# Sparse attention block with expert mixing: the order of the query tiles in the second pass, 4, 7, 5, 6 in place of 7, 4, 6, 5

## The chip, the cores and the metric

The kernel runs on one core of a Trainium2 chip. The metric is the device time of one execution in microseconds (us), the median of several runs. Before the change it is 866.75 us (three runs, 865.97 to 867.92). The engines that matter here are TensorE (PE: matmuls and transposes; its weight loads are the rows PEld), VectorE (DVE), ScalarE (ACT), GpSimd (POOL) and SyncE (SP), whose queue issues the transfers.

## The reference

One block over 1024 tokens of width 512: a layer norm, then the sum of the input, a latent attention with 32 heads and a low-rank expert mix. The attention keeps for each query only the 128 keys that an indexer with 16 heads scores highest.

```python
xn = layernorm(x)                                       # 1024 x 512
q_lat = rmsnorm(xn @ q_a_w) ; q = q_lat @ q_b_w         # 32 heads, 128 plain + 64 rotated
ckv = xn @ kv_a_w ; k_nope, v = rmsnorm(ckv[:, :64]) @ kv_b_w
idx_scores = sum_n iw[n] * relu(iq[n] @ ik.T)           # causal
mask = top_k(idx_scores, 128) & causal                  # one mask for all heads
scores = (q_nope @ k_nope.T + q_pe @ k_pe.T) * 192**-0.5
attn = softmax(where(mask, scores, -inf))
out = x + (attn @ v) @ o_w + sum_e gate[e] * (xn @ A[e].T) @ Bm[e].T * 0.5
```

## The kernel before

The 1024 queries are eight tiles of 128 rows. Causality makes query tile t meet t + 1 blocks of 128 keys, so tile 4 has rows of 640 keys, tile 5 of 768, tile 6 of 896 and tile 7 of 1024. The attention works in latent space: of each head it keeps a 128-wide query (64 latent, 64 rotated) in two float16 parts, high and low, and three products of parts give float32 quality.

The heads go in pairs, 16 pairs. There are two passes over the pairs: the first (half 0, units 0 to 15, steps 0 to 127) does query tiles 0 to 3, the second (half 1, units 16 to 31, steps 128 to 255) tiles 4 to 7. A unit is one pair in one pass and has eight steps: step s of a unit (s = 0 to 7) is head s % 2 of the tile that `ORDERS[half][s // 2]` names. So the list has one entry for two steps, and `tile_of(g)` (L266) is the only way in which it sets widths, and `op` and the index in `out_T` (L767) follow it.

The order of the work is written out by hand, one program for each engine, with semaphores between them. In the second pass, for step g, with the names that the document uses from here on:

- TensorE (loop at L777): S(g+3), the scores of three steps ahead, six matmuls at L731 in one of two score banks; then for an even step T(g), the transposes of its probabilities (L788, one a key block, in two chunks: four blocks, then the rest); then at s = 1 the job R (L647 to L651, five matmuls, the rotated query part of unit u+2), at s = 5 the job L (the same lines, the latent part), at s = 7 the job O (L767, four transposes of the last unit's output); then V, the products with the values (L758, three a key block), of step g-2 for an even step and of step g-4 for an odd one.
- VectorE (loop at L1367): M(g+3), the masked scores with their row minimum of the negated values (L1297, followed by L1302 on odd steps); then P(g), the low parts of T(g)'s chunks (L1075); then R's or L's or O's second reading (L1342, L1075). At s = 4 the last unit's output is scaled (L1313, L1320, L1325).
- ScalarE: the high parts of T(g) (L835), then the exponential of step g+2 (L1024).
- GpSimd: for the odd steps, whose probabilities are transposed by DMA, the split in two parts (L1567, L1569), and the rotation of the queries (L1535, L1540, L1542, L1547), for which SyncE swaps rows by DMA (L425, L426). SyncE issues the DMA transposes (L478) and places the queries (L435).

Three rules tie the engines. S(g) waits until M(g-2) has read the bank (L724). M(g) waits until the probabilities of step g-4 are out of its buffer: for an even step their transposes, for an odd step the low part from GpSimd (L1289 to L1294). And all T chunks, R, L and O go in turn through two banks, psT[0] and psT[1] (`RING`, L327 to L345): each waits until the use before it in its bank has been read (`wait_freed`, L695). A unit has eleven uses: T0a, T0b, R, T2a, T2b, T4a, T4b, L, T6a, T6b, O. So R waits for P of T0a, L for P of T4a, T6b for the reading of L, O for P of T6a, and T0b of the next unit for the reading of O. These numbers after S, M, T, V and P are the step in its unit, and a dash (S0', S3') means the next unit.

Of the kernel before, what the change touches and what calls it, by code (L numbers as in the profile page):

```python
# [47 lines left out]
OUT_S = O_S * WVO_S  # L48
assert HW_S * B_S == OUT_S

ORDERS = ([3, 0, 2, 1], [7, 4, 6, 5])
GROUPS = [[3, 2, 1], [5, 4], [7, 6]]
CH = 512
ARENA = 17024
# [7 lines left out]
def block_kernel(nc, x, wcat, wik, wiq, qbT, wkT, wvT, qpe, ow, bm, qnorm, kvnorm, rbias,  # L62
                 cosq, sinq, cosk, sink, ident_d, causal_d, out):
    with ExitStack() as ctx:
# [192 lines left out]
        def half_of(g):  # L257
            return g // (8 * NP)
# [7 lines left out]
        def tile_of(g):  # L266
            return ORDERS[half_of(g)][g % 8 // 2]

# [268 lines left out]
        def _(pe):  # L537
# [224 lines left out]
            def out_T(bank, u):  # L762
# [3 lines left out]
                for j in range(4):  # L766
                    last = nc.tensor.transpose(bank[:, j * P:(j + 1) * P], op[:, ORDERS[c].index(4 * c + j), :], ident[:])  # L767
                last.then_inc(ot_mm, 1)
# [888 lines left out]
```

## Time and profile before

| | |
|---|---|
| median of three runs | 866.75 us |
| the profiled execution, its own time | 866.68 us |
| its span in the profile | 864.9 us, so 1.8 us lie around it |
| TensorE busy, share of the span | 790.0 us, 91% |
| VectorE busy | 658.2 us, 76% |
| ScalarE busy | 586.3 us, 68% |
| GpSimd busy | 559.8 us, 65% |
| TensorE clock granted | 0.99 of full, mean |

The span is a chain of stages: projections and indexer up to about 285 us, the first pass to about 467 us, the second pass to about 769 us, then the output products. Busy shares are means over all of them. In the timeline a TensorE row "x6" is six matmuls in a row, and its end is modelled: the time that a group takes from its neighbours is the distance from its start to the start of the group behind it. A bracket at the end of a row gives the idle time of the engine ahead of it and what ended it.

### The profile page before, as it was taken

To read this page: it belongs to the slowest core of one execution; us is meant where nothing else is said; L and a number is where in the kernel's file an instruction comes from. 1 tells how busy PE (TensorE), PEld (TensorE's weight loads), DVE (VectorE), ACT (ScalarE), POOL (GpSimd) and SP (SyncE) were. 2 spreads that over 40 slices of the span, in tenths; PEclk is the share of its full clock that TensorE was granted. 3 is DMA by queue.
4 is the path that set the end of the run, shared out by engine and by line. 5 is a ranking of instruction groups with operands and counts; after the bars stand their busy time and mean duration, and the time that the engine had idled before them with its cause. 6 is when DMAs were issued, how large, how long until landed. Compare 5 with 4: busy or idle time off the path is not lost.

```text
span 864.9 us, 20146 instructions
## 1 busy us (share of the span) xinstructions
PE 790.0 (91%) x7432; PEld 489.1 (57%) x7432; DVE 658.2 (76%) x1558; ACT 586.3 (68%) x1325; POOL 559.8 (65%) x478
## 2 busy tenths in 40 slices
PE   4999999978767989898987999999999999999998
PEld 2556545434434555555554677767767767764443
DVE  6367688899998999999998888888887888841000
ACT  3687799979886878888886767666776666740000
POOL 3177398968885676676676788878788888640000
PEclk9999999989999999999999999999999999999999
DMA  8022211213433655655654577777688888861110
GB/s 263 26 74 74 62 55 57 67 25 96 139 109 97 161 136 148 165 135 153 158 147 116 108 152 147 152 152 140 132 147 151 144 154 145 178 129 49 49 49 24
DMA packets 185697, 100.85 MB, mean 117 GB/s; under 512 B 133632, under 2 KB 159616, under 8 KB 185600
## 3 DMA queue, kind: packets, MB, share of 16 engines
q1 hardware_dynamic: 185600, 99.57, 49.9%
q8 instruction: 59, 0.97, 0.5%
q14 instruction: 38, 0.31, 0.1%
HBM read 36.62 MB, written 6.29 MB: 50 GB/s over the span
## 4 chain that ended last, share of the span: by engine, by line
POOL 32%; PE 24%; issue 13%; DVE 12%; DMA 8%; SPq 8%; ACT 3%; POOLq 0%; DVEq 0%; ACTq 0%
PE psS L804 10%; DMA arena<-arena 7%; SPq L478 5%; POOL bias L1516 5%; POOL arena L1542 4%; POOL arena L1540 4%; PE psT L602 4%; POOL arena L1547 3%; PE psS L615 3%; DVE m L1232 3%; POOL ikT L1569 3%; POOL arena L1569 3%; DVE bias L1239 2%; POOL bias L1569 2%; SPq L425 2%
## 5 line engine op out<-in xcount | busy, mean ns | idle before, releaser
L731 PE MATMUL psS<-keyT,arena 128*128 128x512 f16 (+3 forms) x1152 | 230.1, 328 | 7.4 <-DVE small L1297 4.0
L835 ACT ACTIVATE arena<-psT 128x512 f16<-128x512 f32 (+3 forms) x344 | 162.0, 502 | 102.2 <-PE psT L788 64.2
L1297 DVE CUSTOM_DVE_ANT_0 arena<-psS,bias 128x512 f32<-128x512 f32 (+7 forms) x256 | 191.4, 751 | 36.0 <-PE psS L731 16.1
L1024 ACT ACTIVATE arena<-arena,small 128x512 f32<-128x512 f32 (+7 forms) x256 | 197.5, 774 | 29.6 <-DVE small L1297 24.0
L1075 DVE SCALAR_TENSOR_TENSOR arena<-psT,arena 128x512 f16<-128x512 f32 (+3 forms) x262 | 135.2, 536 | 24.4 <-ACT arena L835 23.9
L731 PEld LDWEIGHTS psS<-keyT,arena 128*128 128x128 f16 x1152 | 91.8, 98 | 71.8 <-issue 13.3
L615 PE MATMUL psS<-ikT,big 128*128 128x512 f16 (+3 forms) x528 | 103.8, 341 | 23.0 <-DVE bias L1165 20.9
L788 PE MATMUL psT<-ident,arena 128*128 128x128 f32 x672 | 105.2, 277 | 17.0 <-DVE arena L1075 9.5
L1516 POOL TENSOR_TENSOR bias<-arena,bias 128x768 f32<-128x768 f32 (+2 forms) x48 | 91.4, 1909 | 25.4 <-ACT arena L905 14.7
L788 PEld LDWEIGHTS psT<-ident,arena 128*128 128x128 f32 x672 | 77.3, 141 | 45.0 <-ACT arena L1024 29.1
L615 PEld LDWEIGHTS psS<-ikT,big 128*128 128x128 f16 x528 | 49.3, 100 | 72.3 <-DVE bias L1165 28.4
L1239 DVE MATCH_REPLACE8 bias<-m,bias 128x768 f32<-128x768 f32 (+4 forms) x112 | 89.9, 809 | 0.0
L1232 DVE MAX8 m<-bias 128x8 f32<-128x768 f32 (+4 forms) x112 | 87.5, 816 | 0.5
L1540 POOL TENSOR_TENSOR arena<-arena,sq 128x512 f32<-128x512 f32 x32 | 40.8, 1276 | 65.5 <-DMA arena<-arena 65.5
L758 PEld LDWEIGHTS psO<-val,arena 128*128 128x128 f16 x1728 | 66.1, 98 | 10.7 <-DVE arena L1075 1.6
L758 PE MATMUL psO<-val,arena 128*128 128x64 f16 x1728 | 69.5, 193 | 0.8 <-DVE arena L1075 0.8
L835 ACT ACTIVATE big<-psT 128x512 f16<-128x512 f32 (+1 forms) x64 | 36.2, 566 | 45.4 <-PE psT L767 32.0
L835 ACT ACTIVATE arena<-arena 128x512 f16<-128x512 f32 (+1 forms) x112 | 62.7, 591 | 0.2 <-DMA arena<-in_wiq 0.2
L1422 POOL TENSOR_TENSOR arena<-arena 128x512 f16<-128x512 f32 x32 | 37.5, 1174 | 38.4 <-ACT arena L835 38.4
L1075 DVE SCALAR_TENSOR_TENSOR big<-psT,big 128x512 f16<-128x512 f32 (+1 forms) x64 | 41.8, 653 | 26.8 <-ACT big L835 26.8
L1547 POOL TENSOR_TENSOR arena<-arena 128x512 f16<-128x512 f32 x32 | 37.1, 1160 | 37.4 <-ACT arena L835 37.2
L1165 DVE SCALAR_TENSOR_TENSOR bias<-psS,arena,bias 128x512 f32<-128x512 f32 (+3 forms) x64 | 45.1, 746 | 14.1 <-ACT psS L928 13.6
(165 smaller groups left out, 1404.1 us busy)
## 6 DMA issues: line engine op xcount, KB each, us to landing
arena<-arena SPq DMA_DIRECT2D x192, 128.0 KB, 2.4
arena<-in_wiq SPq DMA_DIRECT2D x32, 256.0 KB, 2.8
arena<-in_ow SPq DMA_DIRECT2D x16, 512.0 KB, 3.8
arena<-in_qbT SPq DMA_DIRECT2D x16, 256.0 KB, 2.5
wvo_parts<-arena SPq DMA_DIRECT2D x16, 256.0 KB, 2.2
arena<-in_qpe SPq DMA_DIRECT2D x16, 128.0 KB, 3.0
arena<-in_x SPq DMA_DIRECT2D x8, 256.0 KB, 2.9
out<-arena SPq DMA_DIRECT2D x8, 256.0 KB, 2.0
```

What stands on the lines that cost most here:

```text
L615: last = mm(bank[:, c:c + w], iq[:, a, n, t * P:(t + 1) * P], ikT[:, b, c:c + w], start=(a, b) == (0, 0), stop=(a, b) == (1, 0))
L731: last = mm(bank[:, k:k + w], Q[:, u % 2, h, a, q:q + P], keyT[:, b, h, k:k + w], start=(a, b) == (0, 0), stop=(a, b) == (1, 0))
L758: last = mm(dst, src[:, a, j * P:(j + 1) * P], val[:, b, j, :], start=j == 0 and n == 0, stop=j == nb - 1 and n == 2)
L788: last = nc.tensor.transpose(bank[:, (j % 4) * P:(j % 4 + 1) * P], pr_of(g)[:, j * P:(j + 1) * P], ident[:])
L804: mm(psS[u][:, 0:CH], big[:, a, n, ds(t * P, P)], wvo[n][:, b, :], start=n == 0 and (a, b) == (0, 0), stop=False)
L835: return nc.scalar.activation(dst, src, ACT.Copy, scale=scale)
L1024: nc.scalar.activation(pr_of(g)[:, 0:kw], pr_of(g)[:, 0:kw], ACT.Exp, bias=shift[:, g % 8:g % 8 + 1], scale=-1.0, accum_out=rsum[:, unit_o ...
L1075: return v.scalar_tensor_tensor(out=dst, in0=src, scalar=scale, in1=hi, op0=ALU.mult, op1=ALU.subtract)
L1232: v.max(m8[:, slot], bias[:, TOFF[t]:TOFF[t + 1]]).then_inc(tk_max, 1)
L1239: v.match_replace(out=row, in_to_replace=m8[:, slot], in_values=row, imm_value=TAKEN).then_inc(tk_rep, 1)
L1297: v.tensor_tensor_reduce(out=pr_of(g)[:, 0:kw], in0=bank[:, 0:kw], in1=bias[:, TOFF[t]:TOFF[t + 1]], scale=-c_s, scalar=3e38, op0=ALU.add, ...
L1516: g.tensor_tensor(row, src[:, 0:P * (t + 1)], row, ALU.add).then_inc(sum_done, 1)
```

## The change

One list changes; every other line is the same.

```diff
-ORDERS = ([3, 0, 2, 1], [7, 4, 6, 5])
+ORDERS = ([3, 0, 2, 1], [4, 7, 5, 6])
```

In the second pass steps 0 and 1 of a unit now have tile 4 (5 key blocks) in place of 7 (8 blocks), steps 2 and 3 tile 7, steps 4 and 5 tile 5, steps 6 and 7 tile 6. The jobs R, L and O keep their steps. Each engine issues the same instructions in all.

On TensorE, ahead of the job O. First before: S1' (tile 7), T6, V4, S2' (tile 4), then O at L767.

```order
L731 MATMUL psS<-keyT,arena 128x512 x6
L788 MATMUL psT<-ident,arena 128x128 x6
L758 MATMUL psT<-val,arena 128x64 x21
L731 MATMUL psS<-keyT,arena 128x512
L731 MATMUL psS<-keyT,arena 128x128
L731 MATMUL psS<-keyT,arena 128x512
L731 MATMUL psS<-keyT,arena 128x128
L731 MATMUL psS<-keyT,arena 128x512
L731 MATMUL psS<-keyT,arena 128x128
L767 MATMUL psT<-ident,arena 128x128 x4
```

The same place of the changed kernel: S1' (tile 4), T6, V4, S2' (tile 7), then O.

```order
L731 MATMUL psS<-keyT,arena 128x512
L731 MATMUL psS<-keyT,arena 128x128
L731 MATMUL psS<-keyT,arena 128x512
L731 MATMUL psS<-keyT,arena 128x128
L731 MATMUL psS<-keyT,arena 128x512
L731 MATMUL psS<-keyT,arena 128x128
L788 MATMUL psT<-ident,arena 128x128 x7
L758 MATMUL psT<-val,arena 128x64 x18
L731 MATMUL psS<-keyT,arena 128x512 x6
L767 MATMUL psT<-ident,arena 128x128 x4
```

The wide scores stood ahead of T6 and now stand behind it, directly ahead of O; the transposes are seven in place of six and the value products 18 in place of 21.

On TensorE, ahead of the job R, before: the last matmul of S3 (tile 4), T0, V6 of the unit before, S4 (tile 6), R's first matmul.

```order
L731 MATMUL psS<-keyT,arena 128x128
L788 MATMUL psT<-ident,arena 128x128 x8
L758 MATMUL psT<-val,arena 128x64 x18
L731 MATMUL psS<-keyT,arena 128x512
L731 MATMUL psS<-keyT,arena 128x384
L731 MATMUL psS<-keyT,arena 128x512
L731 MATMUL psS<-keyT,arena 128x384
L731 MATMUL psS<-keyT,arena 128x512
L731 MATMUL psS<-keyT,arena 128x384
L647 MATMUL psT<-qlT,w1hi 128x512
```

The same place of the changed kernel: S3 (tile 7), T0, V6, S4 (tile 5), R's first matmul.

```order
L731 MATMUL psS<-keyT,arena 128x512 x6
L788 MATMUL psT<-ident,arena 128x128 x5
L758 MATMUL psT<-val,arena 128x64 x21
L731 MATMUL psS<-keyT,arena 128x512
L731 MATMUL psS<-keyT,arena 128x256
L731 MATMUL psS<-keyT,arena 128x512
L731 MATMUL psS<-keyT,arena 128x256
L731 MATMUL psS<-keyT,arena 128x512
L731 MATMUL psS<-keyT,arena 128x256
L647 MATMUL psT<-qlT,w1hi 128x512
```

Between S3 and R the transposes are now five in place of eight and S4 is one key block narrower.

On VectorE, at the turn of a unit, before: M1', P(T6) in two chunks, M2', the reading of O, M3', P(T0).

```order
L1297 ISA arena,small<-psS,bias 128x1024
L1297 ISA small 128x1
L1302 TENSOR_SCALAR small<-small 128x1
L1075 SCALAR_TENSOR_TENSOR arena<-psT,arena 128x512
L1075 SCALAR_TENSOR_TENSOR arena<-psT,arena 128x256
L1297 ISA arena,small<-psS,bias 128x640
L1297 ISA small 128x1
L1075 SCALAR_TENSOR_TENSOR big<-psT,big 128x512
L1297 ISA arena,small<-psS,bias 128x640
L1297 ISA small 128x1
L1302 TENSOR_SCALAR small<-small 128x1
L1075 SCALAR_TENSOR_TENSOR arena<-psT,arena 128x512 x2
```

The same place of the changed kernel.

```order
L1297 ISA arena,small<-psS,bias 128x640
L1297 ISA small 128x1
L1302 TENSOR_SCALAR small<-small 128x1
L1075 SCALAR_TENSOR_TENSOR arena<-psT,arena 128x512
L1075 SCALAR_TENSOR_TENSOR arena<-psT,arena 128x384
L1297 ISA arena,small<-psS,bias 128x1024
L1297 ISA small 128x1
L1075 SCALAR_TENSOR_TENSOR big<-psT,big 128x512
L1297 ISA arena,small<-psS,bias 128x1024
L1297 ISA small 128x1
L1302 TENSOR_SCALAR small<-small 128x1
L1075 SCALAR_TENSOR_TENSOR arena<-psT,arena 128x512
```

The 1024-wide minimum stood ahead of P(T6) and now stands ahead of P(T0).

## Rows read from the trace of the kernel before

**Rows 1.** Windows: busy us and count of each engine, granted clock, DMA share, GB/s
```profile
515.00:735.00 220.00, 218.47 (x2848) 155.19 (x2847) 181.72 (x398) 151.64 (x315) 181.53 (x143) 1.00 0.78 146
```
**Rows 2.** Timeline, VectorE, output scaling of two units: start us, us, instruction
```profile
599.88 0.19 DVE L1313 RECIPROCAL small<-small 128x8 f32<-128x8 f32 x1
600.36 0.69 DVE L1325 TENSOR_TENSOR arena<-psO,small 128x512 f32<-128x512 f32 x1
600.97 1.22 DVE L1297 CUSTOM_DVE_ANT_0 arena<-psS,bias 128x1024 f32<-128x1024 f32 x1
...
619.15 0.69 DVE L1325 TENSOR_TENSOR arena<-psT,small 128x512 f32<-128x512 f32 x1
```
**Rows 3.** Timeline, TensorE, the turn of a unit, from S1' to R
```profile
601.71 1.46 PE L731 MATMUL psS<-keyT,arena 128*128 128x512 f16 x6
603.00 0.82 PE L788 MATMUL psT<-ident,arena 128*128 128x128 f32 x6
603.66 0.78 PE L758 MATMUL psT<-val,arena 128*128 128x64 f16 x21
604.27 0.98 PE L731 MATMUL psS<-keyT,arena 128*128 128x512 f16 x6
605.39 0.66 PE L767 MATMUL psT<-ident,arena 128*128 128x128 f32 x4
...
606.32 0.98 PE L731 MATMUL psS<-keyT,arena 128*128 128x512 f16 x6
607.13 1.04 PE L788 MATMUL psT<-ident,arena 128*128 128x128 f32 x8
...
608.54 1.30 PE L731 MATMUL psS<-keyT,arena 128*128 128x512 f16 x6
609.67 0.38 PE L647 MATMUL psT<-qlT,w1hi 128*128 128x512 f16 x1
```
**Rows 4.** Timeline, VectorE, M ahead of P, tile 7 and tile 6
```profile
603.31 1.23 DVE L1297 CUSTOM_DVE_ANT_0 arena<-psS,bias 128x1024 f32<-128x1024 f32 x1 [0.52 <-PE psS L731]
604.65 1.01 DVE L1075 SCALAR_TENSOR_TENSOR arena<-psT,arena 128x512 f16<-128x512 f32 x2
...
612.81 1.09 DVE L1297 CUSTOM_DVE_ANT_0 arena<-psS,bias 128x896 f32<-128x896 f32 x1 [1.07 <-POOL arena L1569]
...
614.01 0.88 DVE L1075 SCALAR_TENSOR_TENSOR arena<-psT,arena 128x512 f16<-128x512 f32 x2
```
**Rows 5.** Timeline, first pass, a job R that waited for VectorE
```profile
357.72 0.10 PEld L647 LDWEIGHTS psT<-qlT,w1hi 128*128 128x128 f16 x1 [0.62 <-DVE arena L1075]
357.72 0.39 PE L647 MATMUL psT<-qlT,w1hi 128*128 128x512 f16 x1 [0.24 <-DVE arena L1075]
...
357.95 0.38 PE L648 MATMUL psT<-qlT,w1hi 128*128 128x512 f16 x1
```
**Rows 6.** Timeline, where the passes meet: M(128), S(130), O's reading, R
```profile
472.46 1.23 DVE L1297 CUSTOM_DVE_ANT_0 arena<-psS,bias 128x1024 f32<-128x1024 f32 x1
...
473.75 0.99 PE L731 MATMUL psS<-keyT,arena 128*128 128x512 f16 x6 [1.62 <-DVE small L1297]
...
476.07 0.69 DVE L1075 SCALAR_TENSOR_TENSOR big<-psT,big 128x512 f16<-128x512 f32 x1 [0.23 <-ACT big L835]
...
479.12 0.38 PE L647 MATMUL psT<-qlT,w1hi 128*128 128x512 f16 x1
```
**Rows 7.** Timeline, TensorE, the last two jobs O of the second pass's loop
```profile
752.43 0.98 PE L731 MATMUL psS<-keyT,arena 128*128 128x512 f16 x6
753.75 0.66 PE L767 MATMUL psT<-ident,arena 128*128 128x128 f32 x4 [0.34 <-DVE arena L1075]
...
768.21 0.66 PE L767 MATMUL psT<-ident,arena 128*128 128x128 f32 x4 [0.64 <-DVE arena L1075]
```
**Rows 8.** Timeline, GpSimd, the rotation behind its swap, the next split
```profile
601.95 1.27 POOL L1540 TENSOR_TENSOR arena<-arena,sq 128x512 f32<-128x512 f32 x1 [1.75 <-DMA arena<-arena]
...
605.55 1.65 POOL L1569 TENSOR_TENSOR bias<-arena,bias 128x768 f16<-128x768 f32 x1
```

## The prediction

> **What bounds the kernel now.** I read the busy shares of the page first: TensorE leads with 91% over the whole span. Since the list rules the second pass alone, I then read a window inside it: of 220 us TensorE is busy 218.47, at the full granted clock, 1.00, which is the 2.4 GHz level; VectorE is busy 181.72 and GpSimd 181.53 [rows 1]. So TensorE bounds this stage, and the other two have 17% to spare: whether they make it wait depends on where their work stands, not on how much there is. The timeline of VectorE gives the length of a unit: output scaling at 600.36 and at 619.15, 18.79 us apart [rows 2], and all units from 16 to 29 repeat it.
>
> Then I read the timeline of TensorE through the turn of a unit and took each group's cost from its start to the next start. Scores of tile 7 cost 1.29, of tile 4 0.81, of tile 6 1.13, so 0.16 a key block and 0.97 for tile 5; six transposes cost 0.66, so 0.11 a block; 21 value products 0.61, so 0.029 each [rows 3]. The only group that costs more than this is S2' ahead of O: tile 4, but 605.39 - 604.27 = 1.12, so TensorE stands 0.31 us in each unit [rows 3]. What it waits for: O's bank is free when P has read the first chunk of T6, and P stands behind M1' on VectorE. From the end of S1' at 603.00, M1' starts 0.31 later, P 1.34 after that at 604.65; its first chunk of 512 takes 0.69 (the length of such a reading in rows 6), to 605.34; O starts 0.05 later [rows 3, 4]. This chain is 2.39 us long, and TensorE has only 0.66 + 0.61 + 0.81 = 2.08 of work beside it. The difference is the stall.
>
> **The change, part by part.** It issues nothing new: matmuls, readings, exponentials, splits and transfers are as many and as wide. So at best it gives back stalls, and there is 0.31 in a unit. What is to be worked out is each such race in the new order. A chain is 0.31 + M and its turn + 0.69 + 0.05.
>
> O. Ahead of it M1' is now of tile 4. A block costs M 1.23 - 1.09 = 0.14 [rows 4], so three fewer save 0.42 and the chain is 1.97. TensorE has T6 of 7 blocks 0.77, V4 of 18 0.53 and S2' of tile 7 1.29, together 2.59. No stall: the 0.31 goes.
>
> R. It waits for P of T0a, which stands behind M3, now of tile 7: the chain is 2.39. TensorE has T0 of 5 blocks 0.55, V6 of 21 0.61 and S4 of tile 5 0.97: 2.13. It had 0.88 + 0.53 + 1.13 = 2.54, and was not late. So a new stall of 0.26.
>
> L. It waits for P of T4a behind M7, now of tile 6. M to P takes 614.01 - 612.81 = 1.20 [rows 4], the chain 2.25; TensorE has 0.66 + 0.70 + 0.81 = 2.17 (T4 of 6, V2 of 24, S0' of tile 4). A new stall of 0.08.
>
> T6b. It waits for VectorE's reading of L, which now comes late: behind S7 the chain is 0.31 + 1.20, P(T4) 0.93 or less, the output scaling 600.97 - 599.88 = 1.09 [rows 2], M0' of tile 4 0.74, the reading 0.69 and 0.05, together 5.01. TensorE needs 2.17 + 0.08 + 1.08 + 0.44 + 0.81 + 0.44 = 5.02. That is a dead heat; I take 0.02 for it and keep 0 and 0.1 as its ends.
>
> A stalled start. Does TensorE lose more than the wait when it restarts? In the first pass one R waited for VectorE: weight load and matmul both start at 357.72, and the next matmul 0.23 later, where 0.22 is usual [rows 5]. I take 0.01 at most, inside the rounding above. The Trainium skill, "TensorE: Matmul & The Clock Gate", section "Architectural detail: the array is 16× 32×32, not 1× 128×128", says that the queue pulls weight loads ahead of running matmuls, but also that a matmul can begin before its weight load is complete. By the first half alone each new stall would pay one more load, the 0.10 of rows 5, and the sum would be some 2.7 us higher; the row is with the second half.
>
> Waits that go but give nothing: VectorE idles 1.07 ahead of M5 for GpSimd's split of step 1 [rows 4]. With tile 4 in place of 7 there the split is done before its scores are; TensorE did not wait for this M, since S7 comes later. The next things late are R and L, as above.
>
> Per unit: 0.26 + 0.08 + 0.02 = 0.36 in place of 0.31. Over the pass: before, 14 stalls of 0.31 (units 16 to 29) and one of 753.75 - 752.43 - 0.81 = 0.51 in unit 30 [rows 7], together 4.85. After, R in units 17 to 29, 13 x 0.26 = 3.4, and L with T6b in units 16 to 29, 14 x 0.10 = 1.4; unit 30 has neither R nor L, and its O isn't late. Together 4.8: a gain of 0.05, nothing.
>
> Where the passes meet. S(128) starts as before but is 0.48 shorter, which brings the first pass's last readings, the masks and M(128) forward, and M(128) is 0.42 shorter: S(130), at 473.75 before [rows 6], starts at 472.85. Then S(130) and S(131) are of tile 7. Step 127 belongs to the first pass, where the readings come ahead of the next M, so M(130) stands behind the reading of O. O ends at 472.85 + 1.29 + 0.22 + 0.44 = 474.80; ScalarE and the reading add some 0.8 and 0.6, to 476.2 (476.07 + 0.6 before [rows 6]); M(130) takes 1.14 and M(131) with its turn 1.34, to 478.7; P(T0a) 0.69 and 0.05: R starts at 479.4, a full 1.0 us after TensorE is ready, where before it started at 479.12 [rows 6]. Up to R the new order has done less: 2 x 0.81 + 2 x 1.29 + 0.97 + 0.55 = 5.72 against 2 x 1.29 + 2 x 0.81 + 1.13 + 0.88 = 6.21. So it is 0.3 + 0.49 = 0.8 us behind. I take 0.8, with 0 and 1.4 as ends (a reading more or less in the way).
>
> The end. The last O waited 0.64 for VectorE behind two exponentials [rows 7], of tile 5; they are of tile 6 now, a block wider each, and one evacuation is a block narrower: 0.1 to 0.3, I take 0.2. The four value products of late steps are as long in all, and what comes behind them is untouched.
>
> **The sum**, against the profiled execution's own 866.68 us (span 864.9 and 1.8 around it, 0.07 under the median, so no correction): 866.68 - 0.05 + 0.8 + 0.2 = 867.6 us.
>
> **The rivals.**
> *A, the stall is simply gone.* If R and L hide after all, the pass gives back 4.85: 866.68 - 4.85 + 1.0 = 862.8 us. For it: VectorE and GpSimd idle, and O's is the only stall of a steady unit. Against it: the chain into R is the very chain of rows 3 and 4, and the work beside it is 0.26 too short, whatever the load.
>
> *B, slower by GpSimd's loop.* The rotation waits for its swap by DMA, which stands behind the transposes of step 3 on SyncE's queue, now of tile 7 in place of 4. It started at 601.95, 4.37 ahead of S3' at 606.32; the split of step 7 ended at 607.20 [rows 8], and M3' was due at 606.32 + 0.81 + 0.31 = 607.44: 0.24 to spare. The split is a block wider now, about 0.4, and M3' due 0.48 later, so 0.3 to spare. It decides from the point where the rotation starts less than 4.1 us ahead of S3'; from there M3' and so R are late by each further tenth, in 13 units. For it: the transposes are 8 blocks in place of 5 just ahead of the swap. Against it: those of step 1 are 5 in place of 8, also ahead of the swap, so its queue holds the same in all. At 0.25 a unit: 867.6 + 3.3 = 870.9 us.
>
> *C, the races are lost by more.* Each new stall costs 0.1 more (a restart, or T6b late): 27 x 0.1 = 2.7, 870.3 us. Rows 5 speak against it, the dead heat at T6b for it.
>
> *D, nothing moves:* the place where the passes meet costs nothing, 866.8 us. It lies in the forecast's own range.
>
> **How the numbers follow.** The bound from which this kernel can be told from no change is 0.2%, 1.7 us: faster is under 865.0, slower over 868.5. Forecast with D 0.63, of which 0.05 reaches over 868.5; A 0.10, which half of a stall saved would already fulfil; B 0.14; C 0.13, of which 0.04 stays under 868.5. Faster 0.10, same 0.62, slower 0.28 (0.05 + 0.14 + 0.09). The forecast's own range is 866.2 to 868.6 by its unknowns. For 8 in 10 the range reaches to 865.2, the near side of A, and to 870.7, taking in most of B and C.
>
> **What would show it.** Right: in the timeline of TensorE the group ahead of O costs 1.29 with no wait, R starts 0.2 to 0.3 late behind S4 and L 0.1 late behind S0'; the unit is 18.8 to 18.9 long; the first R of the pass waits about 1 us; VectorE no longer waits for GpSimd at M5. Wrong: a unit of 18.5 (A), one over 19.0 with M3' waiting for GpSimd (B), or gaps at T6b (C).

## The result and the profile after

| | before | after |
|---|---|---|
| median of 20 runs each | 867.68 us (865.95 to 869.95) | 870.27 us (867.97 to 873.37) |
| ratio after / before | | 1.0035, 95% interval 1.0023 to 1.0047 |
| profiled execution, its span | 866.68, 864.9 us | 867.97, 866.2 us |

The change costs 0.35%, 3.0 us by the ratio (the medians differ by 2.6). The forecast was 867.6 us and no difference that can be told. By the prediction's own bound of 868.5 us this is slower, for which it gave 0.28; the time lies in its wide range (865.2 to 870.7), near the slow end, and outside the forecast's own (866.2 to 868.6).

The profiled execution is the quickest of the 20 of the changed kernel. Its span is only 1.3 us longer than before's, largely because S(128) happens to start 1.0 us earlier in it (466.40 against 467.41, behind a first pass that is the same code). So I compare from S(128) to the first output product (L804), which is what the change touches, and cut this stretch at two jobs R. R stands at the same place of each unit, so the distance between two of them (a period) is one unit:

| us | before | after | after, profiled again (e9) | forecast |
|---|---|---|---|---|
| S(128) to the first R, unit 16 | 11.71 | 12.51 (+0.80) | 12.80 (+1.09) | +0.3 |
| that R to the R of unit 29, 13 periods | 243.30 | 244.88 (+1.58) | 245.11 (+1.81) | +0.65 |
| to the first output product | 46.72 | 46.54 (-0.18) | 46.54 (-0.18) | 0.0 |
| sum | 301.73 | 303.93 (+2.20) | 304.45 (+2.72) | +0.95 |

(Of the forecast's 0.8 at the meeting of the passes, 0.49 is work left over at R. It falls due in the last line, where it meets the stalls that go there.)

The window that answers to [rows 1], then TensorE in the turn of a steady unit after, from S2' to R, which answers to [rows 3].

```profile
515.00:735.00 220.00, 217.75 (x2834) 153.09 (x2832) 180.43 (x397) 152.09 (x313) 179.98 (x141) 1.00 0.77 147
```

```profile
622.41 1.46 PE L731 MATMUL psS<-keyT,arena 128*128 128x512 f16 x6
623.70 0.60 PE L767 MATMUL psT<-ident,arena 128*128 128x128 f32 x4
...
624.84 1.46 PE L731 MATMUL psS<-keyT,arena 128*128 128x512 f16 x6
626.13 0.71 PE L788 MATMUL psT<-ident,arena 128*128 128x128 f32 x5
626.68 0.78 PE L758 MATMUL psO<-val,arena 128*128 128x64 f16 x21
627.29 1.14 PE L731 MATMUL psS<-keyT,arena 128*128 128x512 f16 x6
628.52 0.39 PE L647 MATMUL psT<-qlT,w1hi 128*128 128x512 f16 x1
...
647.73 0.39 PE L647 MATMUL psT<-qlT,w1hi 128*128 128x512 f16 x1 [0.48 <-DVE arena L1075]
```

O starts 1.29 behind S2' of tile 7, as long as such a group is: no stall. S4 of tile 5 is worth 0.97 and R starts 1.23 behind it: the stall of 0.26, to the hundredth. R of this unit and R of the last are 18.82 apart (609.70, 628.52), and so are nine of the thirteen periods, where 18.84 was forecast. The first is 17.85 (17.82 before), since the first R comes late. Three are longer: 19.21, 19.17 and 19.25. The last row above belongs to the first of these. The next rows are GpSimd and VectorE at the turn of the steady unit, then of the late one: rotation, split of step 7, M3'.

```profile
620.58 1.28 POOL L1540 TENSOR_TENSOR arena<-arena,sq 128x512 f32<-128x512 f32 x1 [2.06 <-DMA arena<-arena]
...
624.28 1.90 POOL L1569 TENSOR_TENSOR arena<-arena 128x896 f16<-128x896 f32 x1
...
626.45 1.23 DVE L1297 CUSTOM_DVE_ANT_0 arena<-psS,bias 128x1024 f32<-128x1024 f32 x1 [0.60 <-PE psS L731]
...
640.03 1.28 POOL L1540 TENSOR_TENSOR arena<-arena,sq 128x512 f32<-128x512 f32 x1 [2.69 <-DMA arena<-arena]
...
643.66 1.46 PE L731 MATMUL psS<-keyT,arena 128*128 128x512 f16 x6
643.73 1.89 POOL L1569 TENSOR_TENSOR ikT<-arena,ikT 128x896 f16<-128x896 f32 x1
...
645.66 1.23 DVE L1297 CUSTOM_DVE_ANT_0 arena<-psS,bias 128x1024 f32<-128x1024 f32 x1 [0.99 <-POOL ikT L1569]
```

In the steady unit the rotation starts 4.26 ahead of S3' (624.84), the split ends at 626.18, and M3' waits for its scores, as always 0.60. In the late unit the swap's data come later, the rotation starts 3.63 ahead of S3', the split ends at 645.62, and M3' starts right behind it, 0.39 late; R is late by the same 0.39. This is rival B's mechanism, in 3 periods of 13: 0.39 + 0.35 + 0.43 = 1.2 us (1.4 in e9, in the same three periods).

It is there before the change too, where it costs nothing. Timeline of the kernel before, VectorE and GpSimd, with S3' of the late unit: first a unit on time, then a late one (701.80 is another).

```profile
608.85 1.29 DVE L1075 SCALAR_TENSOR_TENSOR arena<-psT,arena 128x512 f16<-128x512 f32 x2 [0.38 <-ACT arena L835]
...
640.07 1.27 POOL L1540 TENSOR_TENSOR arena<-arena,sq 128x512 f32<-128x512 f32 x1 [2.29 <-DMA arena<-arena]
...
643.66 1.65 POOL L1569 TENSOR_TENSOR ikT<-arena,ikT 128x768 f16<-128x768 f32 x1
643.90 0.98 PE L731 MATMUL psS<-keyT,arena 128*128 128x512 f16 x6
...
645.35 0.82 DVE L1297 CUSTOM_DVE_ANT_0 arena<-psS,bias 128x640 f32<-128x640 f32 x1 [0.37 <-POOL ikT L1569]
...
646.43 1.29 DVE L1075 SCALAR_TENSOR_TENSOR arena<-psT,arena 128x512 f16<-128x512 f32 x2
...
701.80 0.82 DVE L1297 CUSTOM_DVE_ANT_0 arena<-psS,bias 128x640 f32<-128x640 f32 x1 [0.45 <-POOL ikT L1569]
```

M3' of tile 4 takes 0.82, and behind it P(T0) waits 0.38 for ScalarE anyway. A late M3' eats this wait (646.43 has none) and R is on time. With tile 7 in its place M3' takes 1.23, P(T0) comes straight behind it, and R with it: a late M3' is paid in full, in all three late units.

### The profile page after: what moved, and what is told of

It reads as the page before. It is cut to its first block, busy times and chain, and to the rows that moved or that the text cites. A ratio compares the mean times of both kernels' runs of the same rounds, so it can differ in the third digit from the quotient of the medians.

```text
span 866.2 us, 20146 instructions
## 1 busy us (share of the span) xinstructions
PE 792.4 (91%) x7432; PEld 488.2 (56%) x7432; DVE 658.7 (76%) x1558; ACT 587.6 (68%) x1325; POOL 560.8 (65%) x478
## 4 chain that ended last, share of the span: by engine, by line
PE 47%; DVE 24%; issue 10%; POOL 9%; ACT 6%; SPq 2%; DMA 2%; DVEq 0%; POOLq 0%; ACTq 0%
PE psS L731 12%; PE psS L804 10%; DVE arena L1297 5%; DVE m L1232 5%; POOL bias L1516 5%; PE psT L788 4%; DVE bias L1239 4%; PE psT L602 4%; DVE arena L1075 3%; PE psO L758 3%; ACT arena L835 3%; PE psS L615 3%; PE psT L758 3%; ACT arena L1024 2%; DVE bias L1165 2%
## 5 line engine op out<-in xcount | busy, mean ns | idle before, releaser
L1297 DVE CUSTOM_DVE_ANT_0 arena<-psS,bias 128x512 f32<-128x512 f32 (+7 forms) x256 | 191.8, 752 | 42.7 <-PE psS L731 38.2
L1540 POOL TENSOR_TENSOR arena<-arena,sq 128x512 f32<-128x512 f32 x32 | 40.8, 1276 | 70.9 <-DMA arena<-arena 70.9
L1422 POOL TENSOR_TENSOR arena<-arena 128x512 f16<-128x512 f32 x32 | 37.5, 1174 | 37.7 <-ACT arena L835 37.7
L1394 DVE SCALAR_TENSOR_TENSOR arena<-psS,arena 128x512 f32<-128x512 f32 x8 | 5.4, 689 | 62.3 <-PE psS L809 62.3
```

What stands on the lines that cost most here:

```text
L1297: v.tensor_tensor_reduce(out=pr_of(g)[:, 0:kw], in0=bank[:, 0:kw], in1=bias[:, TOFF[t]:TOFF[t + 1]], scale=-c_s, scalar=3e38, op0=ALU.add, ...
```

## Where the passes meet, after

Timeline of the changed kernel: S(128), GpSimd's rotation of that place, the two masks, M(128), S(130), the first R; it answers to [rows 6].

```profile
466.40 0.97 PE L731 MATMUL psS<-keyT,arena 128*128 128x512 f16 x6 [2.33 <-DVE small L1297]
...
468.06 1.26 POOL L1542 TENSOR_TENSOR arena<-arena 128x512 f32<-128x512 f32 x1
...
468.74 2.63 DVE L1249 TENSOR_SCALAR bias<-bias 128x1024 f32<-128x1024 f32 x2
469.41 1.48 POOL L1555 TENSOR_TENSOR arena<-arena 128x512 f16<-128x512 f32 x1
...
471.41 0.82 DVE L1297 CUSTOM_DVE_ANT_0 arena<-psS,bias 128x640 f32<-128x640 f32 x1
...
472.30 1.47 PE L731 MATMUL psS<-keyT,arena 128*128 128x512 f16 x6 [0.45 <-DVE small L1297]
...
478.91 0.39 PE L647 MATMUL psT<-qlT,w1hi 128*128 128x512 f16 x1 [0.78 <-DVE arena L1075]
```

The same place before.

```profile
467.41 1.46 PE L731 MATMUL psS<-keyT,arena 128*128 128x512 f16 x6 [2.33 <-DVE small L1297]
...
469.11 1.27 POOL L1542 TENSOR_TENSOR arena<-arena 128x512 f32<-128x512 f32 x1
...
470.23 2.20 DVE L1249 TENSOR_SCALAR bias<-bias 128x1024 f32<-128x1024 f32 x2
470.46 1.49 POOL L1555 TENSOR_TENSOR arena<-arena 128x512 f16<-128x512 f32 x1
```

The masks start 2.82 behind S(128) before and 2.34 after: the 0.48 of the forecast is there. But M(128) starts 5.05 and 5.01 behind it: the masks took 0.43 longer and the 0.48 was lost again. R then came 0.52 later than the forecast's 479.4 - 467.41 = 11.99. Their single durations say why. The group of L1249 by itself, after and before:

```profile
L1249 DVE TENSOR_SCALAR bias<-bias x2: 1140/1356/1573, 468.7 to 469.8; 128x1024 f32<-128x1024 f32 x1, 128x896 f32<-128x896 f32 x1
```

```profile
L1249 DVE TENSOR_SCALAR bias<-bias x2: 700/1140/1579, 470.2 to 470.8; 128x1024 f32<-128x1024 f32 x1, 128x896 f32<-128x896 f32 x1
```

In both traces each mask ends nearly the same time behind the end of the GpSimd operation that runs when it starts. After: L1542 ends at 469.32, the 1024-wide mask at 468.74 + 1.14 = 469.88, 0.56 later; L1555 ends at 470.89, the second at 471.37, 0.48 later. Before: L1542 ends at 470.38, the first mask at 470.23 + 0.70 = 470.93, 0.55 later; L1555 ends at 471.95, the second at 472.43, 0.48 later. So the masks do some 1.0 us of work and wait for GpSimd through the rest, 1.2 before and 1.6 after. GpSimd's operations stand where they stood against S(128) (L1542 starts 1.70 behind it before and 1.66 after; what comes ahead of both is the first pass, which is unchanged). So masks that start 0.48 sooner only wait longer, and M(128) comes no earlier. The Trainium skill, "SBUF — State Buffer", section "Who interferes with whom", has VectorE and GpSimd share one pair of ports: where a VectorE instruction runs in a 2-port mode, as a `tensor_scalar` can, or has two SBUF inputs while the GpSimd instruction reads SBUF, the second one to issue is blocked until the first is done. The traces agree in all four places (0.56, 0.48, 0.55 and 0.48 us behind the end of the GpSimd operation), though no row shows in which mode a mask ran. In the other direction L1555 takes 1.48 after and 1.49 before, where a mask is still running at its start, and 1.16 in e9, where none is.

## The experiments

After the result I had one theory in two parts. The late splits cost 1.2 us or more, because M3' is now followed straight by the chain into R. The place where the passes meet costs 1.3 or more. The rivals: the swap by DMA and its queue as such; the dead heat at T6b (rival C); and that both parts are chance of one profile. The medians of the kernel before, measured beside each of these runs, lie between 867.2 and 867.5.

**e1 and e2: the swap taken out** of the second pass (from unit 18 on the rotated query part lacks it), in the new and in the old order.

```diff
-                if s == 3 and u + 2 < NU:
+                if s == 3 and u + 2 < NU and u < NP:
                     swap(u + 2)
...
-                pool.wait_ge(sw_done, 32 * u + 32)
+                if u < NP + 2:
+                    pool.wait_ge(sw_done, 32 * u + 32)
```

> The changed kernel without the row swaps by DMA in the second pass (from unit 18 on GpSimd multiplies what stands in its buffer and waits for no swap, so the rotated query part is wrong; its instructions are as many). Theory 1 (the split of step 7 comes late when the swap lands late, and the new order pays all of it): M3' waits for GpSimd in no unit, every unit of the pass is 18.82 us long, and the time falls from 870.3 by 2 to 3 us, to 867.3 to 868.3, with the runs closer together. Theory 2 (the loss lies where the passes meet and in the new waits of R and L): 870 us, no change but for a few tenths.

> The same left out of the kernel before. Theory 1 says that the old order has some 0.4 us to spare behind M3' (P of T0 waits for ScalarE there), so late swaps cost it little: 866 to 867.5, at most 1.5 us under the kernel before. Theory 2: the same as the kernel before, 867.7. If it falls by as much as the changed kernel does, lateness of the swap is no difference between the two orders.

Measured: e1 874.29 us, ratio 1.0091 (1.0076 to 1.0106); e2 867.86, ratio 1.0005 (0.9996 to 1.0014). Of what was expected of e1 only one thing came true: M3' is late in no unit. Yet from unit 18 on every unit takes 19.28. e2 lies where its second theory had it (867.7) and not in the range of the first (866 to 867.5): by the times alone, e1 and e2 say nothing for the late splits. Timeline of e1, GpSimd and VectorE at the output scaling (this kernel's L1541 is the rotation, L1540 elsewhere), and TensorE at T6b of another unit.

```profile
568.93 0.69 DVE L1075 SCALAR_TENSOR_TENSOR arena<-psT,arena 128x512 f16<-128x512 f32 x1
...
569.68 0.55 PE L788 MATMUL psT<-ident,arena 128*128 128x128 f32 x3 [0.27 <-DVE arena L1075]
...
585.48 1.27 POOL L1541 TENSOR_TENSOR arena<-arena,sq 128x512 f32<-128x512 f32 x1
...
586.15 0.62 DVE L1320 TENSOR_TENSOR small<-small 128x8 f32<-128x8 f32 x1
586.87 0.69 DVE L1325 TENSOR_TENSOR arena<-psT,small 128x512 f32<-128x512 f32 x1
```

Without its wait the rotation starts right behind the split of step 5 and lies over VectorE's smallest operation, 128x8 with both inputs in SBUF. This takes 0.62 in place of 0.17 and ends with the rotation (586.77 and 586.75), in this unit and in twelve more. Behind it the output scaling, M0' and the reading of L come 0.45 later, and T6b, whose race the forecast called a dead heat, is lost by the whole of it: 18.82 + 0.46 = 19.28. In the old order the same edit costs nothing (L1320 is held in no unit of e2). So rival C is no part of the changed kernel (its L1320 is 0.17 in every unit, and its units on time are 18.82), but 0.45 of delay there is enough for it.

**e3 and e4: which part of the pass.** The new order in unit 16 alone (e3), and in all units but 16 (e4).

```diff
+OTHER = [4, 7, 5, 6]        # e3, beside the old ORDERS; e4: the other way round
+        def order_of(u):
+            if u == NP:
+                return OTHER
+            return ORDERS[u // NP]
```

> The new order in unit 16 alone, the old one from unit 17 on. It pays what the place costs where the passes meet, and neither the waits of R and L nor the late splits of 13 units. Theory 2 in its part for the meeting of the passes (traces: R of unit 16 starts 0.8 us later and 0.49 us of work is still to do): 1.3 us over the kernel before, of which the work left may come back where the orders change (the next unit then starts with tile 7). So plus 0.8 to plus 1.3 us. If only the steady units cost, plus 0.

> The old order in unit 16, the new one from unit 17 on. It leaves out the cost where the passes meet and keeps everything else. Theory 1: 1.5 to 2 us over the kernel before, so about 1 us under the changed kernel. Theory 2: within 0.5 us of the kernel before.

Measured: e3 869.18, ratio 1.0017 (1.0005 to 1.0028); e4 868.35, ratio 1.0020 (1.0009 to 1.0030). That is 1.5 and 1.7 us, together 3.2 of 3.0. From S(128) to the first product the profile of e3 has 303.26, 1.5 more than before, and units of 18.79 from the third of the pass on. That of e4 has 11.70 up to the first R, as before, and four late units, 19.47, 19.04, 19.89 and 19.18. These are its M3' (L1303 is L1297 elsewhere).

```profile
645.19 1.23 DVE L1303 CUSTOM_DVE_ANT_0 arena<-psS,bias 128x1024 f32<-128x1024 f32 x1 [1.24 <-POOL ikT L1575]
...
683.05 1.23 DVE L1303 CUSTOM_DVE_ANT_0 arena<-psS,bias 128x1024 f32<-128x1024 f32 x1 [0.81 <-POOL arena L1575]
...
702.94 1.23 DVE L1303 CUSTOM_DVE_ANT_0 arena<-psS,bias 128x1024 f32<-128x1024 f32 x1 [1.67 <-POOL ikT L1575]
...
722.12 1.22 DVE L1303 CUSTOM_DVE_ANT_0 arena<-psS,bias 128x1024 f32<-128x1024 f32 x1 [0.95 <-POOL bias L1575]
```

What they wait over the usual 0.60 is 0.64 + 0.21 + 1.07 + 0.35 = 2.3, and the four units are 2.3 longer than four of 18.82. Both parts are clear of noise, and by the medians they add.

**e5: the late splits alone taken away.** The subtraction of step 7 covers half its columns in the second pass; so the low parts of the rest are not computed.

```diff
+                lw = kw // 2 if half_of(x) and x % 8 == 7 else kw
-                g.tensor_tensor(rows_of_turn(d)[:, kw:2 * kw], pr_of(x)[:, 0:kw], rows_of_turn(d)[:, 0:kw],
+                g.tensor_tensor(rows_of_turn(d)[:, kw:kw + lw], pr_of(x)[:, 0:lw], rows_of_turn(d)[:, 0:lw],
```

> The changed kernel in which GpSimd's subtraction of step 7 (L1569) covers half of the columns in the second pass, 448 of 896, so it ends about 0.9 us sooner and the low parts of the rest are stale. The swap, the rotation and their times stay. Theory 1 (late splits ahead of M3' are the part of the loss that is neither in the meeting of the passes nor in the steady waits): M3' waits for GpSimd in no unit or in one, the time falls from 870.3 by about 1.5 us, to 868.5 to 869.2. Theory 3 (the steady unit itself loses it, by holds of VectorE while GpSimd runs): no change, 870.

Measured: 869.01 (866.78 to 869.11), ratio 1.0018 (1.0009 to 1.0026). All periods behind the first are 18.82 to 18.84, and no M3' waits for GpSimd. Against 1.0035 that is 1.5 us back (the two intervals overlap a little): the price of the late splits, by an edit that changes no other instruction. From S(128) to the first product its profile has 302.81 us, 1.1 and 1.6 less than the two of the changed kernel.

**e6: the swap issued earlier**, ahead of the transposes of step 3, nothing left out.

```diff
+                if s == 3 and u + 2 < NU and u >= NP:
+                    swap(u + 2)
                 if s and turns(g):
                     turn(g)
```

> The changed kernel with SyncE's swap of step 3 issued ahead of the DMA transposes of that step in place of behind them; nothing is left out. The rotation then no longer waits for the swap and starts right behind the split of step 5. By the trace of e1 this puts GpSimd's L1540 on top of VectorE's L1320, which then takes 0.62 in place of 0.17 us, and T6b, which I had called a dead heat, is late by that: units of 19.28, 874 us. If e1's slowness came from the missing transfers and not from the rotation's place, this kernel is at 868, the changed kernel without its late splits.

Measured: 873.68, ratio 1.0079 (1.0063 to 1.0096), units of 19.27 or 19.28 from unit 17 on, L1320 held to 0.61 or 0.62 in 13 of them. As expected: an earlier rotation is in time for the split and in the way of the output scaling. So the rotation may come neither later (the split of step 7) nor much earlier (the output scaling).

**e7 and e8: the order of M and P turned where the race is.** In e7 the first chunk of P(T0) goes ahead of M3'. In e8, from the kernel before, the first chunk of P(T6) goes ahead of M1' (`s in (6,)`).

```diff
-                if half_of(g):
+                ahead = half_of(g) and s in (0,)
+                if half_of(g) and not ahead:
                     next_max(g + AHEAD)
                 for use in uses_of(g):
                     what, at, c = use
+                    if ahead and use == ("T", g, 1):
+                        next_max(g + AHEAD)
```

> The changed kernel with one move on VectorE: in the second pass at s = 0 the first chunk of P(T0) goes ahead of M3'. If the chain through M3 is what R waits for, R waits no more: 13 x 0.26 and the 1 us of the first R, and M3' starts 1.5 us later, so that late splits are hidden: 870.3 - 3.4 - 1.0 - 1.5 = 864.4 us. If R's wait isn't the chain through M3, 870.

> The kernel before with the same kind of move: in the second pass at s = 6 the first chunk of P(T6) goes ahead of M1'. If the chain through M1' is what O waits for, its 0.31 us in each unit goes: 14 x 0.31 + 0.5 = 4.8 us less, 862.8 us, with units of 18.48 us. If not, 867.6.

Measured: e7 865.36, ratio 0.9979 (0.9970 to 0.9989); e8 874.34, ratio 1.0084 (1.0070 to 1.0097). Timeline of e7, VectorE and R:

```profile
607.23 0.69 DVE L1075 SCALAR_TENSOR_TENSOR arena<-psT,arena 128x512 f16<-128x512 f32 x1 [1.55 <-ACT arena L835]
...
607.84 1.22 DVE L1297 CUSTOM_DVE_ANT_0 arena<-psS,bias 128x1024 f32<-128x1024 f32 x1
...
608.10 0.38 PE L647 MATMUL psT<-qlT,w1hi 128*128 128x512 f16 x1
...
609.70 1.14 PE L731 MATMUL psS<-keyT,arena 128*128 128x512 f16 x6
```

VectorE had been idle 1.55; P goes there, M3' comes straight behind it, and R has no wait. The units are 18.56, which is 18.82 less the 0.26 of R; and since P no longer stands behind M3', a late split is hidden again up to the last periods (one of 19.01). The first R comes 11.79 behind S(128) in place of 12.51, 0.7 less, where 1.0 was expected. The same idea in e8 was expected at 862.8 and came out 11.5 us slower, with units of 19.28. Timeline of e8, VectorE and TensorE:

```profile
606.63 0.69 DVE L1075 SCALAR_TENSOR_TENSOR arena<-psT,arena 128x512 f16<-128x512 f32 x1 [1.48 <-ACT arena L835]
607.24 1.22 DVE L1297 CUSTOM_DVE_ANT_0 arena<-psS,bias 128x1024 f32<-128x1024 f32 x1
...
607.89 0.60 PE L758 MATMUL psT<-val,arena 128*128 128x64 f16 x15
...
608.52 0.99 PE L731 MATMUL psS<-keyT,arena 128*128 128x512 f16 x6
...
609.34 0.61 PE L788 MATMUL psT<-ident,arena 128*128 128x128 f32 x4
...
610.38 0.66 PE L788 MATMUL psT<-ident,arena 128*128 128x128 f32 x4 [0.43 <-DVE big L1075]
```

The stall of O went, but M1' comes later and ends at 608.46, and S3' waits for its bank: 0.63 behind 15 products that are worth 0.44, so 0.19. Then T0b waits for the reading of O, which stands behind M1' and M2': 1.04 behind T0a, worth 0.44, so 0.60. Together 0.79 lost for 0.31 saved, and 18.79 + 0.48 is the unit. It isn't the idle time of VectorE that sets the two apart: ahead of P it is 1.55 in e7 and 1.48 in e8. What differs is the work that TensorE has until it needs the M that was put back, and what stands behind this M on VectorE. In e7 M3' ends at 609.06, and S5, which needs its bank, comes at 609.70, behind the five matmuls of R (1.08); in e8 M1' ends at 608.46, and S3' stands ready behind O, which is worth only 0.44. And behind M1' comes the reading of O, for which T0b waits.

**e9: the changed kernel once more**, a single execution.

> The changed kernel once more, for a second profile of it. Theory 1: the part of the pass beyond units of 18.82 us is the sum of the late M3' waits, some 0.4 us each; this sum differs from execution to execution and accounts for the difference of the two profiled spans, once the start of the second pass is set equal. If instead all units are of some other length, theory 1 is wrong about the spread.

Measured: 871.15 us, span 869.4, 3.2 longer than the first profile. The late M3' sum to 1.4 in place of 1.2, so 0.2 of the 3.2. Of the rest, 1.0 lies ahead of S(128), 0.3 between S(128) and R, and 1.7 behind the pass, from the first product to the end (97.55 against 95.87). That the spread of the times comes from the late splits is not borne out: nine tenths of this difference lie outside them.

**e10 and e11: the two masks moved** from ahead of M(128) in step 125 to behind M(126) in step 123, in the new and in the old order.

```diff
                 if g == 8 * NP:
-                    for t in GROUPS[2]:
-                        mask(t)
                     dve.wait_ge(mask_done, 7)
                 if g < STEPS:
                     row_max(g)
+                if g == 8 * NP - 2:
+                    for t in GROUPS[2]:
+                        mask(t)
```

> The changed kernel with the two masks (L1249) of tiles 7 and 6 moved from step 125 to the end of step 123, where VectorE stood idle for 2.10 us. In the new order S(130) waits only 0.45 us for M(128) behind the masks, and R waits for M(131), which follows S(131): the gain is 0.4 to 0.6 us, 870.3 - 0.5 = 869.8.

> The same move in the kernel before. There S(130) waited 1.62 us for M(128), and nothing later is waited for: 1.5 us less, 867.3 - 1.5 = 865.8. If both orders gain alike, the wait for the masks isn't what sets them apart where the passes meet.

Measured: e10 869.50, ratio 1.0021 (1.0009 to 1.0032); e11 866.88, ratio 0.9991 (0.9982 to 0.9999). S(128) to R is 11.89 in e10, against 12.51 and 12.80, and 11.57 in e11, against 11.71. So the masks did hold M(128) back in the new order: without them R comes 11.89 behind S(128), and the forecast had 11.99. The new order gets 0.6 to 0.9 us back here by the profiles and 1.2 by the ratios (whose intervals overlap), more than the 0.5 expected. The old order gets 0.8 by its ratio where 1.5 was expected, and its interval all but reaches 1; its profile shows only 0.14 here, but with the clock lower behind S(128), which it was not before (against e2, where it was, 0.38). The two gains can't be told apart by the times. With the masks moved in both, the new order is 0.32 behind the old at R, where the forecast had 0.3.

**e12: e7 and e10 together**, the new order with P ahead of M3' and the masks early.

> The new order with both moves, the first chunk of P(T0) ahead of M3' and the masks at step 123. The gains add where nothing new comes late: e7 at 865.4 less 0.5 to 1.6 (with P ahead the first R no longer waits for M(131), so the whole wait of S(130) can come back, and no more): 864.3 us.

Measured: 864.76 (863.66 to 867.32), ratio 0.9973 (0.9962 to 0.9984), the lowest median of these runs, 2.3 us under the old order and 5.4 under the new. From e7 (ratio 0.9970 to 0.9989) it can't be told, so that the two gains add is not shown. Its window:

```profile
515.00:735.00 220.00, 219.75 (x2891) 156.75 (x2890) 183.60 (x407) 156.64 (x318) 178.77 (x140) 1.00 0.80 149
```

TensorE does 2,891 matmuls in the 220 us, where it did 2,848 before and 2,834 after the change, and 2,890 in e7.

## Why the prediction was wrong

*What bounds the second pass, and the steady unit: right.* O's stall is gone, R's is 0.26 as forecast, L's 0.09 (617.84 to 618.74 is 0.90, where S0' is worth 0.81) for 0.08, and the wait of M5 for GpSimd is gone without any gain. The unit is 18.82 for 18.84: T6b's race is won, or lost by no more than the rows can tell. That it came out so near was in part luck: the forecast had called this race a dead heat, and a delay of 0.45 there is lost in full (e1, e6). A stalled start costs nothing beyond the wait: weight load and matmul of R start together at 647.73. A change that takes a stall of 0.31 away made the unit 0.03 longer, where the forecast had 0.05.

*The step that failed first: "0.3 to spare", and rival B at 0.14.* The mechanism, its place and its price in time were right: it begins at about 4.0 us between rotation and S3' (forecast 4.1), and 3.63 gives 0.39. Wrong was the margin, read from one unit [rows 8] and used for thirteen. The rotation's start moves with the landing of its swap. In the trace of before its wait for that transfer runs from 0.43 to 2.36 us, its start lies 3.76 to 5.68 us ahead of S3' in fourteen units, and two of its M3' wait for the split. They were to be read there: 643.90 - 640.07 = 3.83 is one of the two, 3.76 the other, so by the forecast's own 4.1 two units would have cost 0.3 each. Nobody pays for them before, since P(T0) waits 0.38 for ScalarE, and the new order takes this cover away. So B was no case of its own, in all units or in none, but a term of the sum, 3 units of 13 at 0.4. It measured 1.2 and 1.4 in profiles and 1.5 by e5, where the forecast had 0 in its sum (and 3.3 us in all thirteen units as rival B).

*The second: where the passes meet, mis-sized.* Forecast 0.8 (0.3 at R and 0.49 of work left). Measured 0.80 at R, which with the 0.49 is 1.3, 1.6 in the second profile, and 1.5 by e3. The mechanism was the forecast's: two M of tile 7 with the reading of O ahead of them, and R 0.78 late [after, 478.91], for 1.0 forecast. What failed is the step "which brings the masks and M(128) forward": the masks are held by GpSimd's operations, and these don't come forward. The clock has a share too. In e9 and e3 TensorE fell to the lower level at the very start of S(128) (1.76 long there, 0.97 after), the masks start 3.43 behind it and take 1.84 and 1.82, and R comes 12.80 and 12.78 behind it. In the profile after, in e1, e5 and e6 the level fell 1 us or more later, and R comes 12.51 to 12.53 behind it. So 0.3 of e9's 1.6 goes with the earlier fall. And e1 and e2, the two orders with one and the same edit and the fall in the same place, differ at R by 12.53 - 11.95 = 0.58 and not by 0.80, so some 0.2 of the first profile's difference may be the clock's as well.

*The end: some 0.15 better than forecast.* The last O waits 0.73 after and 0.64 before [rows 7], 0.1 more where the forecast had 0.2.

```profile
769.13 0.66 PE L767 MATMUL psT<-ident,arena 128*128 128x128 f32 x4 [0.73 <-DVE arena L1075]
```

*The sum by these.* 0.95 forecast, + 0.5 for the meeting, + 1.2 for late splits, - 0.3 for the unit's 0.02 in 13 periods, - 0.15 for the end is 2.2, the first profile's difference. With 1.4 and 0.8 for the first two it is 2.7, the second's. The runs say 3.0, and e3 and e4 together 3.2.

*The rivals.* A (the stall simply gone): refuted by the steady units, 18.82 where it needs 18.5. C (races lost by more): not in this kernel, but e1 and e6 show how near it lies. D (nothing moves where the passes meet): refuted by e3 (1.0005 to 1.0028). B: above.

*Open:* why the swap lands later in some units than in others (the same three in both profiles of the changed kernel, other ones in part before), and how much the lower clock costs the new order where the passes meet, since no profile has the new order there without it.

## What to carry to other kernels

A reordering that takes a stall away moves the slack as well: ask of each engine that was late "sometimes, at no cost" what hid it, and whether that cover stays. Read a margin that hangs on a transfer from all the repetitions in the trace, never from one, and put what its tail costs into the sum. Where a wide operation stands ahead of a short one in a chain, turning the two can give more than this order of the tiles could (e7) or cost more (e8). Idle time of the engine ahead of them doesn't decide it: work out who needs the operation that is put back, and what stands behind it.

## What the runs showed of the hardware

- A VectorE operation with both inputs in SBUF (128x8, float32) took 0.61 to 0.63 us in place of 0.17 beside a GpSimd operation that had started first, and ended 0.01 to 0.03 behind it (e1 and e6, 13 units each). With one input in PSUM it was not held: M takes 0.81 to 0.83 at 640 columns and 1.21 to 1.23 at 1024, whether a GpSimd operation runs at its start or not.
- A 1024-wide float32 `tensor_scalar` in SBUF ended 0.55 or 0.56 us behind the GpSimd operation that it found running and took 0.70 (before) and 1.14 (after); the 896-wide one ended 0.48 behind it and took 1.58 and 1.57. In e9, with no GpSimd operation running when it started, the 896-wide one took 0.61.
- TensorE fell to the lower clock level, 1.2 GHz, within 1.5 us of the start of S(128) in all nine profiles with the new order there, and in two of five with the old (e2, e11). It had stood idle 2.33 ahead of S(128) in all of them. Windows from 466 to 472 us (columns as in [rows 1]), after and then before:

```profile
466.00:472.00 6.00, 5.46 (x34) 2.92 (x34) 4.91 (x9) 2.43 (x6) 5.09 (x4) 0.72 0.08 30
```

```profile
466.00:472.00 6.00, 4.59 (x34) 2.68 (x34) 4.11 (x9) 2.97 (x9) 4.09 (x4) 1.00 0.17 52
```

The granted clock is 0.72 of full as a mean over this window after, and 1.00 before. Two profiles of the old order, with the fall (e2) and without it (before), differ by 0.24 between S(128) and R, 11.95 and 11.71. What decides whether it falls, and when, stays open.
